# Counting edges between matmuls: two rings of one-hots and a new order of the three engines

## The chip, the cores and the metric

The kernel runs on one core of a Trainium2 chip. The metric is the device time of one execution in microseconds (us). Its engines are named as in the profile: PE is TensorE, DVE is VectorE, ACT is ScalarE, POOL is GpSimd, SP is SyncE, which issues most transfers.

## What is computed

Four graph layers over 1250 nodes with 512 features and 20000 edges `src -> dst`, `dst` sorted and dense at low numbers. Each layer normalises, aggregates over edges and multiplies by weights; two of them do so twice, so there are six convolutions (L0, L1A, L1B, L2, L3A, L3B).

```python
edge_index = jnp.stack([src, dst])
h = jnp.maximum(_layernorm(x, axis=-1), 0.0)
x = x + _L0_gnn_ref(h, edge_index, ...)   # relu(mean over edges of h @ W_l.T + b_l + h @ W_r.T)
h = jnp.maximum(_layernorm(x, axis=-1), 0.0)
x = x + _L1_gnn_ref(h, edge_index, ...)   # two convolutions
h = jnp.maximum(_layernorm(x, axis=-1), 0.0)
x = x + _L2_gnn_ref(h, edge_index, ...)
h = jnp.maximum(_layernorm(x, axis=-1), 0.0)
x = x + _L3_gnn_ref(h, edge_index, ...)   # two convolutions
return x
```

## The kernel before

The sum over edges is a product with a matrix of counts, nodes by nodes: entry (d, s) is how many edges go from s to d. The kernel builds this matrix once, while it also computes the two products of L0, and then aggregates six times with it.

**Counting.** The receivers are cut into 20 windows of 64 nodes, named (b, h): tile b of 128 nodes (0 to 9), h is 0 or 1. The 20000 sorted edges lie in 157 tiles of 128 edges. One stretch of counting is one window: `count(b, h)` on TensorE visits the tiles of edges that hold its receivers, in groups of six (RING): for each of the six, two matmuls of 320 columns take a one-hot of receivers (`dst_hot`, 128 columns: the window's nodes, once for the lower and once for the upper half of the senders) against a one-hot of senders (`src_hot`, 640 columns). The number of groups comes from a table, `tiles_of`, that the kernel computes itself; each engine loads a window's entry into a register (`visits_of`, the TENSOR_LOAD of line 254) and keeps in a register `visited` how many edge tiles are done. There are 35 groups: 6 and 3 in windows (0,0) and (0,1), two in each window of tiles 1 to 4, one in each of tiles 5 to 9. A window's counting begins with two matmuls of zeros (L1150) and ends with one (L1164).

Three engines share a group. VectorE (`givers`, L753 to L762) makes the six `src_hot` and the last two `dst_hot`; ScalarE (`receivers`, L486 to L496) the first four `dst_hot`, as 1 - |node - receiver| cut at zero: four times `apart` (L491), then one instruction over all four (L496). There is one ring of six buffers: `hot_used` counts the buffers that TensorE has read, and both makers wait for it. ScalarE's `counts_of` (L464) then moves the counts out of their two PSUM banks (4 and 5 for h = 0, 6 and 7 for h = 1) into `count16`, and SyncE transposes them by DMA into `countT16`.

**L0's products.** Per node tile b: ScalarE `deviation` (L477), VectorE `features` (normalised z, L781 and L788), TensorE `turn` (four transposes into PSUM, L1173), ScalarE `hi` (L514) and VectorE `lo` (L801) (the transposed features split into two parts), TensorE `first_p` (twelve matmuls, the neighbour product) and `first_q` (twelve, the own product, both L1180), ScalarE `phi` (L520) and VectorE `p_rest` (L808) (the product p split into two parts), VectorE `first_own` (L814). `statistics` (L735, L740, L744) are those of the next tile's rows.

**The order** is written out by hand for each engine; every engine runs in its own order and waits on semaphores. For tile b from 2 on, `merged(b, r)` has, on

- PE: count(b,0), first_p(b-1), turn(b), count(b,1), first_q(b-1)
- DVE: givers(b,0), features(b), first_own(b-2), givers(b,1), lo(b), statistics(b+1), p_rest(b-1)
- ACT: deviation(b), receivers(b,0), counts_of(b,0), receivers(b,1), hi(b), phi(b-1), counts_of(b,1)

in loops over pairs of tiles; tiles 0 and 1 come before the loop, mixed with the turning and splitting of L0's weights (`turn_first`, `split_first`). SyncE's list `order` has the transposes of tiles 0 and 1, the load of W1l into `wstage` (the weights of L1A, for which ScalarE waits at the start of L0's aggregation, L457), then the transposes of tiles 2 to 9, then three rows of vectors. After the last products the kernel reads one value (`big`) and branches; L0's aggregation is `aggregate` (L1259): 20 matmuls per tile against `cstage`, which ScalarE's `stage` (L529) writes for tile i + 2 when tile i is aggregated.

The wait that ties ScalarE's receivers to the ring:

```python
act.wait_ge(first_rows, n + RING)
for e in range(BY_ACT):
    last = nc.scalar.activation(apart[:, e:e + 1, :], tab[:, window(b, h), :], ACT.Abs, scale=-1.0,
                                bias=nodeT[:, 0, bass.ds(t + e, 1)])
last.then_inc(apart_done, RING)
act.wait_ge(apart_done, n + RING)
act.wait_ge(hot_used, n + BY_ACT)
nc.scalar.activation(dst_hot[:, 0:BY_ACT, :], apart[:, :, :], ACT.Relu, scale=-1.0,
                     bias=1.0).then_inc(first_rows, RING)
```

Of the kernel before, what the change touches and what calls it, by code (L numbers as in the profile page):

```python
# [13 lines left out]
P = 128  # L14
# [24 lines left out]
def gnn_kernel(nc, ins, out):  # L39
# [49 lines left out]
    wstage, _ = place("wstage", [P, KF, D], F32)  # L89
# [28 lines left out]
    apart, _ = place("apart", [P, BY_ACT, P], BF16, place.end)  # L118
# [35 lines left out]
    def p_bank(s, r):  # L154

        return PP if s == L0 else PP + r

    def q_bank(s, r):

        return PP + 1 if s == L0 else QQ + r  # L160
# [19 lines left out]
    givers_ready, hot_used = sem("givers_ready"), sem("hot_used")  # L180
    first_rows, ones_set = sem("first_rows"), sem("ones_set")
    apart_done, nodes_placed = sem("apart_done"), sem("nodes_placed")
# [69 lines left out]
    def visits_of(engine, visited, b, h):  # L252
# [4 lines left out]
        n0 = engine.snap(visited, min_val=0, max_val=NW * (ETP + RING))  # L257
# [3 lines left out]
        engine.reg_mov(visited, n1)  # L261
# [19 lines left out]
    with nc.Block() as block:  # L281

        @block.sync
        def _(sp):
# [15 lines left out]
            order = [("f", 0), ("f", 1), ("f", 2), ("v", rows[0]), ("v", rows[1]), ("t", 0), ("t", 1), loads[0]]  # L300
            order += [("t", b) for b in range(2, NT)]
# [127 lines left out]
        def _(act):  # L429
# [13 lines left out]
            act.sem_inc(first_rows, RING)  # L443
# [36 lines left out]
            visited = act.alloc_register("act_visited")  # L480
            act.reg_mov(visited, 0)

            def receivers(b, h):

                n0, n1, offset = visits_of(act, visited, b, h)
                with act.Fori(n0, n1, RING) as n:  # L486

                    t = tile_at(act, n, offset)
                    act.wait_ge(first_rows, n + RING)
                    for e in range(BY_ACT):  # L490
                        last = nc.scalar.activation(apart[:, e:e + 1, :], tab[:, window(b, h), :], ACT.Abs, scale=-1.0,  # L491
                                                    bias=nodeT[:, 0, bass.ds(t + e, 1)])
                    last.then_inc(apart_done, RING)
                    act.wait_ge(apart_done, n + RING)
                    act.wait_ge(hot_used, n + BY_ACT)
                    nc.scalar.activation(dst_hot[:, 0:BY_ACT, :], apart[:, :, :], ACT.Relu, scale=-1.0,  # L496
                                         bias=1.0).then_inc(first_rows, RING)
# [11 lines left out]
            def hi(s, i, r):  # L509
# [4 lines left out]
                nc.scalar.activation(hT_hi[:, r, :, :], ps[:, HT + r, :].rearrange("p (k n) -> p k n", k=KF),  # L514
# [22 lines left out]
            receivers(0, 0)  # L537
            split_first(0, range(2, KF))
            receivers(0, 1)
            counts_of(0, 0)  # L540
            split_first(1, range(0, 2))
            deviation(0, 0)
            deviation(0, 1)
            receivers(1, 0)
            counts_of(0, 1)
            split_first(1, range(2, KF))
            receivers(1, 1)
            counts_of(1, 0)
            hi(L0, 0, 0)
            phi(L0, 0, 0)  # L550
            hi(L0, 1, 1)
            counts_of(1, 1)
# [11 lines left out]
            with act.Fori(2, NT - 1, 2) as b0:  # L564
                for k in range(2):
                    merged(b0 + k, k)

# [739 lines left out]
```

## Time and profile before

| | |
|---|---|
| median of 3 runs | 703.03 us (702.97 to 704.32) |
| profiled execution | 705.11 us, span 703.3 us |
| TensorE busy | 662.6 us, 94% of the span |
| VectorE busy | 401.7 us, 57% |
| ScalarE busy | 283.1 us, 40% |
| counting and L0's products | from the start to 171.44 us |
| mean granted TensorE clock | 0.990 |

The span is the time from the first to the last instruction of the profiled execution; the device time of the same execution is 1.8 us more. A busy share near 100% over the whole span says nothing about one stage: the page's 40 slices have TensorE at 5 to 9 tenths in the first ten slices and at 9 from there on. A row of the timeline gives start, duration, instruction and, in brackets, how long the engine sat idle before it and whose work ended that. The array's matmuls overlap: twelve counting matmuls have a busy time of 1.80 us, but what follows can start 1.66 us after their start.

### The profile page before, as it was taken

The page shows a single profiled execution, that of the slowest core. Times are in us where ns is not written, and L with a number is a line of the kernel's source. Part 1 is how long each engine was busy: PE and PEld are TensorE (multiplying, and loading weights), DVE is VectorE, ACT ScalarE, POOL GpSimd, SP SyncE. Part 2 cuts the span into 40 slices and gives each one's busy share as a digit, 9 for nine tenths or more (in the row PEclk, how much of TensorE's full clock was granted, in tenths as well). Part 3 has the DMA queues.
Part 4 walks back from the last instruction along what each step waited for, and adds up shares of the span by engine and source line. Part 5 has one row for each costly group of instructions (what it writes and reads, how often), then busy time and mean ns, then how long its engine had stood idle before and what let it go on. Part 6 is the DMA issues. An engine that isn't in the chain of part 4 may idle for free.

```text
span 703.3 us, 11458 instructions
## 1 busy us (share of the span) xinstructions
PE 662.6 (94%) x3199; PEld 527.5 (75%) x3200; DVE 401.7 (57%) x911; ACT 283.1 (40%) x522; POOL 18.1 (3%) x25
## 2 busy tenths in 40 slices
PE   5878888988999999999999999999999999999997
PEld 3436566766888888888888888888877778887786
DVE  6986787674566444133434567554899861156323
ACT  4864665664341123563223332223553352223321
POOL 2000000000000000000000000000321000000000
PEclk9989999999999999999999999999999999999999
DMA  6213101113055000210000210000200000000011
GB/s 225 79 20 88 21 19 28 30 36 82 35 158 105 0 0 2 75 60 1 0 0 2 75 61 0 0 0 4 75 1 0 0 3 0 0 1 0 32 61 56
DMA packets 26273, 25.22 MB, mean 36 GB/s; under 512 B 14076, under 2 KB 17972, under 8 KB 26232
## 3 DMA queue, kind: packets, MB, share of 16 engines
q1 hardware_dynamic: 24952, 22.12, 11.2%
q10 hardware_dynamic: 1280, 2.56, 1.1%
q8 instruction: 24, 0.39, 0.2%
q14 instruction: 17, 0.14, 0.1%
HBM read 17.20 MB, written 4.20 MB: 30 GB/s over the span
## 4 chain that ended last, share of the span: by engine, by line
PE 80%; DVE 7%; issue 6%; ACT 3%; DVEq 2%; ACTq 0%; DMA 0%; SPq 0%
PE ps L1259 36%; PE ps L1180 33%; PE ps L1159 7%; PE ps L1173 3%; DVE src_hot L762 2%; DVE stats L735 1%; ACT cstage L529 1%; DVE own L994 1%; ACT dst_hot L496 1%; ACT apart L491 1%; PE ps L1121 1%; DVEq L762 0%; DVE mv_now L740 0%; DVE hT_lo L801 0%; DVE dst_hot L760 0%
## 5 line engine op out<-in xcount | busy, mean ns | idle before, releaser
L1259 PE MATMUL ps<-p_hi,cstage 128*128 128x512 f32 x600 | 235.7, 393 | 5.7 <-ACT cstage L529 2.9
L1259 PE MATMUL ps<-p_lo,cstage 128*128 128x512 f32 x600 | 234.6, 391 | 0.0
L1180 PE MATMUL ps<-w_hi,hT_hi 128*128 128x512 f32 x400 | 162.3, 406 | 3.4 <-DVE hT_lo L801 3.3
L1180 PE MATMUL ps<-w_hi,hT_lo 128*128 128x512 f32 x400 | 156.7, 392 | 0.0
L1180 PE MATMUL ps<-w_lo,hT_hi 128*128 128x512 f32 x400 | 156.2, 390 | 0.0
L1259 PEld LDWEIGHTS ps<-p_hi,cstage 128*128 128x128 f32 x600 | 113.2, 189 | 30.9 <-issue 7.3
L1259 PEld LDWEIGHTS ps<-p_lo,cstage 128*128 128x128 f32 x600 | 113.3, 189 | 23.1
L966 DVE SCALAR_TENSOR_TENSOR own<-ps,nodal,own 128x512 f32 (+1 forms) x60 | 44.9, 749 | 123.0 <-PE ps L1259 122.6
L529 ACT CAST cstage<-countT 128x1280 fp32r (+1 forms) x50 | 62.6, 1263 | 89.1 <-PE ps L1259 88.4
L1180 PEld LDWEIGHTS ps<-w_hi,hT_hi 128*128 128x128 f32 x400 | 75.2, 188 | 19.8 <-DVE hT_lo L801 2.9
L1159 PE MATMUL ps<-src_hot,dst_hot 128*128 128x320 bf16 x420 | 68.7, 315 | 22.2 <-ACT dst_hot L496 12.3
L1180 PEld LDWEIGHTS ps<-w_hi,hT_lo 128*128 128x128 f32 x400 | 75.1, 188 | 16.5
L1180 PEld LDWEIGHTS ps<-w_lo,hT_hi 128*128 128x128 f32 x400 | 75.4, 188 | 13.9
L762 DVE TENSOR_SCALAR src_hot<-iota,nodeT 128x640 bf16<-128x640 f16 x210 | 71.5, 381 | 15.1 <-PE ps L1159 8.8
L1159 PEld LDWEIGHTS ps<-src_hot,dst_hot 128*128 128x128 bf16 x420 | 38.6, 102 | 47.9 <-DVE src_hot L762 32.0
L514 ACT ACTIVATE hT_hi<-ps 128x512 fp32r<-128x512 f32 x60 | 35.7, 594 | 73.7 <-PE ps L1173 73.5
L808 DVE TENSOR_TENSOR p_lo<-ps,p_hi 128x512 f32 (+1 forms) x40 | 27.6, 691 | 59.0 <-ACT p_hi L520 58.9
L520 ACT ACTIVATE p_hi<-ps 128x512 f32 (+1 forms) x40 | 23.9, 597 | 72.4 <-PE ps L1180 72.4
L801 DVE SCALAR_TENSOR_TENSOR hT_lo<-ps,hT_hi 128x512 fp32r<-128x512 f32 x60 | 41.0, 684 | 13.5 <-ACT hT_hi L514 13.3
L491 ACT ACTIVATE apart<-tab,nodeT 128x128 bf16 (+1 forms) x140 | 44.8, 391 | 9.7 <-issue 5.5
L477 ACT ACTIVATE nodal<-mv,eps (+1 forms) x40 | 11.7, 294 | 67.4 <-DVE mv L744 67.4
L1173 PE MATMUL ps<-ident,z 128*128 128x128 f32 x240 | 36.0, 272 | 0.2 <-DVE z L788 0.2
(117 smaller groups left out, 450.8 us busy)
## 6 DMA issues: line engine op xcount, KB each, us to landing
x<-in_x ACTq DMA_DIRECT2D x1, 2304.0 KB
out_x<-x SPq DMA_DIRECT2D x9, 256.0 KB
wstage<-in_L_gnn_W SPq DMA_DIRECT2D x2, 1024.0 KB, 5.2
swap<-count SPq DMA_DIRECT2D x2, 800.0 KB, 8.6
count<-swap SPq DMA_DIRECT2D x2, 800.0 KB, 8.1
wstage<-in_L_gnn_W_l SPq DMA_DIRECT2D x2, 512.0 KB, 4.2
w_own<-in_L_gnn_W_r SPq DMA_DIRECT2D x1, 1024.0 KB, 11.2
vec<-in_L_gnn_b SPq DMA_DIRECT2D x4, 256.0 KB, 7.7
```

What stands on the lines that cost most here:

```text
L491: last = nc.scalar.activation(apart[:, e:e + 1, :], tab[:, window(b, h), :], ACT.Abs, scale=-1.0, bias=nodeT[:, 0, bass.ds(t + e, 1)])
L514: nc.scalar.activation(hT_hi[:, r, :, :], ps[:, HT + r, :].rearrange("p (k n) -> p k n", k=KF), ACT.Relu).then_inc(hi_done, 1)
L520: nc.scalar.activation(p_hi[:, bass.ds(i, 1), :], ps[:, p_bank(s, r), :], ACT.Copy, scale=1.0 if CONVS[s]["own"] else dis[:, bass.ds(i, 1) ...
L529: nc.scalar.copy(stage_of(s, r), columns(s, i)).then_inc(stage_ready, 1)
L762: nc.vector.tensor_scalar(src_hot[:, e, 0:NS], iota[:, :], nodeT[:, 1, bass.ds(t + e, 1)], None, ALU.is_equal).then_inc(givers_ready, 1)
L801: nc.vector.scalar_tensor_tensor(hT_lo[:, r, :, :], ps[:, HT + r, :].rearrange("p (k n) -> p k n", k=KF), 0.0, hT_hi[:, r, :, :].bitcast(F ...
L808: nc.vector.tensor_tensor(p_lo[:, bass.ds(i, 1), :], ps[:, p_bank(s, r), :], p_hi[:, bass.ds(i, 1), :].bitcast(F32), ALU.subtract).then_in ...
L966: nc.vector.scalar_tensor_tensor(own_, ps[:, AGG + r:AGG + r + 1, :], scale[:, bass.ds(i, 1)], own_, ALU.mult, ALU.add).then_inc(t_done, 1)
L1159: last = nc.tensor.matmul(ps[:, COUNT + 2 * h + k, 0:NS // 2], dst_hot[:, e, :], src_hot[:, e, k * (NS // 2):(k + 1) * (NS // 2)], start=F ...
L1173: last = nc.tensor.transpose(ps[:, HT + r, k * P:(k + 1) * P], z[:, r, k * P:(k + 1) * P], ident[:, :])
L1180: last = nc.tensor.matmul(ps[:, bank, :], a[:, r, k, :], w[:, slot, k, :], start=n == 0, stop=n == len(pairs) - 1)
L1259: last = nc.tensor.matmul(ps[:, AGG + r, :], cstage[:, part, k, :], p_[:, k, :], start=n == 1, stop=n == 2 * len(parts) * NT)
```

## The change

- `src_hot`, `dst_hot` and `apart` exist twice, and so do the semaphores `givers_ready`, `hot_used`, `first_rows`, `apart_done` and the register `visited`: windows with h = 0 use ring 0, windows with h = 1 ring 1. Ring 1's `src_hot` lies in `wstage`.
- The orders are rewritten. A step `merged` and a step `merged_end` make one tile; both end with the one-hots of the window after. `statistics` comes in its three parts, with the load from the table behind the first; elsewhere the load stands behind z, counts or ahead of the product.
- ScalarE moves a window's counts out after it has made the receivers of the next window, and `phi` and `p_rest` come one tile later.
- L0's PSUM banks: p has banks 1 and 2 by turns, q has bank 3, the turned features bank 0 alone; `turn` waits `lo` of the tile before, `first_p(i)` waits `p_rest(i-2)`.
- SyncE loads W1l after all transposes.
- Tiles 8 and 9 are written out behind the loop on all three engines (before: on VectorE alone).

```diff
-    src_hot, _ = place("src_hot", [P, RING, NS], BF16, cstage_at)
-    dst_hot, _ = place("dst_hot", [P, RING, P], BF16, place.end)
+    src_hot, dst_hot, apart = [None, None], [None, None], [None, None]
+    src_hot[0], _ = place("src_hot0", [P, RING, NS], BF16, cstage_at)
+    dst_hot[0], _ = place("dst_hot0", [P, RING, P], BF16, place.end)
+    apart[0], _ = place("apart0", [P, BY_ACT, P], BF16, place.end)
     assert place.end <= cstage_at + 2 * NT * P * 4
+    src_hot[1], _ = place("src_hot1", [P, RING, NS], BF16, wstage_at)
+    assert place.end <= wstage_at + KF * D * 4
+    dst_hot[1], _ = place("dst_hot1", [P, RING, P], BF16, own_at + 9 * D * 4)
...
-            order = [("f", 0), ("f", 1), ("f", 2), ("v", rows[0]), ("v", rows[1]), ("t", 0), ("t", 1), loads[0]]
-            order += [("t", b) for b in range(2, NT)]
+            order = [("f", 0), ("f", 1), ("f", 2), ("v", rows[0]), ("v", rows[1])]
+            order += [("t", b) for b in range(NT)] + loads[:1]
...
             def merged(b, r):
 
                 deviation(0, b)
-                receivers(b, 0)
+                counts_of(b - 1, 1)
+                found = visits_of(act, visited, b, 1)
+                phi(L0, b - 2, r)
+                receivers(b, 1, found)
                 counts_of(b, 0)
-                receivers(b, 1)
+
+            def merged_end(b, r):
+
+                found = visits_of(act, visited, b + 1, 0)
                 hi(L0, b, r)
-                phi(L0, b - 1, 1 - r)
-                counts_of(b, 1)
+                receivers(b + 1, 0, found)
...
+            givers(0, 1, visits_of(dve, visited, 0, 1))
             dve.wait_ge(x_loaded, 32)
-            statistics(0, 0)
+            statistics_1(0, 0)
+            found = visits_of(dve, visited, 1, 0)
+            statistics_2(0, 0)
+            statistics_3(0, 0)
             split_first(1, range(0, 2))
-            statistics(0, 1)
+            givers(1, 0, found)
             features(L0, 0, 0)
-            givers(1, 0)
...
             def merged(b, r):
 
-                givers(b, 0)
                 features(L0, b, r)
+                found = visits_of(dve, visited, b, 1)
+                p_rest(L0, b - 2, r)
                 first_own(b - 2)
-                givers(b, 1)
+                givers(b, 1, found)
+
+            def merged_end(b, r):
+
+                statistics_1(0, b + 1)
+                found = visits_of(dve, visited, b + 1, 0)
+                statistics_2(0, b + 1)
+                statistics_3(0, b + 1)
                 lo(L0, b, r)
-                if not (isinstance(b, int) and b == NT - 1):
-                    statistics(0, b + 1)
-                p_rest(L0, b - 1, 1 - r)
+                givers(b + 1, 0, found)
...
+            def merged(b, r):
+                found = visits_of(pe, visited, b, 1)
                 first_p(b - 1, 1 - r)
                 turn(L0, b, r)
-                count(b, 1)
+                count(b, 1, found)
...
+                found = visits_of(pe, visited, b + 1, 0)
                 first_q(b - 1, 1 - r)
+                count(b + 1, 0, found)
```

In the order of instructions two places matter. The first is ScalarE's, in the loop over tile pairs, from `hi` to the load ahead of the next window's receivers (names: `apart_79` below is the first of the two `apart`). Before:

```order
L514 ACTIVATE hT_hi<-ps 128x512
L519 REGISTER_ALU
L520 ISA
L520 ACTIVATE p_hi<-ps 128x512
L463 REGISTER_ALU
L464 ISA
L464 ACTIVATE count_49,deg_win<-ps 128x640
L477 ISA
L477 ACTIVATE nodal<-mv,eps 128x1
L254 ISA
L254 TENSOR_LOAD tiles_of
L257 ISA
```

And in the changed kernel, from `counts_of(b, 0)` on:

```order
L474 ACTIVATE count_49,deg_win<-ps 128x640
L263 ISA
L263 TENSOR_LOAD tiles_of
L266 ISA
L525 ACTIVATE hT_hi<-ps 128x512
L497 UNCONDITIONAL_BRANCH
L497 ISA
L502 ISA
L502 REGISTER_ALU
L502 ISA
L502 ACTIVATE apart_79<-tab,nodeT 128x128
```

Between `hi` of a tile and the first receivers of the next tile stood p_hi, the counts of (b,1), the deviation and the load; now nothing stands there but the branch into the ring's loop.

The second is VectorE's, in the same loop, from `lo` to the next tile's first one-hot of senders. Before:

```order
L801 SCALAR_TENSOR_TENSOR hT_lo<-ps,hT_hi 128x512
L735 ISA
L735 BN_STATS stats<-x 128x6
L738 REGISTER_ALU
L740 BN_AGGR mv_now<-stats 128x2
L744 ISA
L744 TENSOR_SCALAR mv<-mv_now 128x2
L808 ISA
L808 TENSOR_TENSOR p_lo<-ps,p_hi 128x512
L254 REGISTER_ALU
L254 TENSOR_LOAD tiles_of
L257 ISA
```

In the changed kernel:

```order
L759 BN_STATS stats<-x 128x6
L263 ISA
L263 TENSOR_LOAD tiles_of
L266 ISA
L764 BN_AGGR mv_now<-stats 128x2
L768 REGISTER_ALU
L768 TENSOR_SCALAR mv<-mv_now 128x2
L825 REGISTER_ALU
L826 SCALAR_TENSOR_TENSOR hT_lo<-ps,hT_hi 128x512
L778 UNCONDITIONAL_BRANCH
L778 ISA
L787 REGISTER_ALU
```

Statistics and the load moved ahead of `lo`, and `p_lo` went to the step `merged`, behind `features`.

## Rows read from the trace of the kernel before

**Rows 1.** Windows of the trace: busy time of each engine, granted clock, DMA share, GB/s

```profile
20.00:36.00 16.00, 13.31 (x90) 7.40 (x88) 15.50 (x54) 13.15 (x35) 0.00 (x0) 1.00 0.11 34
...
42.00:44.00 2.00, 1.36 (x6) 0.79 (x7) 1.23 (x5) 1.78 (x5) 0.00 (x0) 0.50 0.05 8
...
62.00:160.00 98.00, 86.66 (x521) 64.33 (x522) 73.56 (x234) 61.99 (x159) 0.00 (x0) 1.00 0.17 36
```

**Rows 2.** Waits up to 170 us: total us, times, longest

```profile
PE ps L1159 <- ACT dst_hot L496: 12.3, 11, 4.9
DVE hT_lo L801 <- ACT hT_hi L514: 12.1, 5, 2.8
PE ps L1159 <- DVE src_hot L762: 9.2, 11, 1.1
```

**Rows 3.** Timeline of TensorE, tiles 4 to 6: start, us, instruction, idle before

```profile
103.65 1.80 PE L1159 MATMUL ps<-src_hot,dst_hot 128*128 128x320 bf16 x12 [0.57 <-ACT dst_hot L496]
...
109.30 1.80 PE L1159 MATMUL ps<-src_hot,dst_hot 128*128 128x320 bf16 x12 [0.91 <-DVE src_hot L762]
...
114.52 1.80 PE L1159 MATMUL ps<-src_hot,dst_hot 128*128 128x320 bf16 x12
...
119.00 0.23 PE L1150 MATMUL ps<-zeros 128*128 128x64 bf16 x2
120.31 1.80 PE L1159 MATMUL ps<-src_hot,dst_hot 128*128 128x320 bf16 x12 [1.07 <-DVE src_hot L762]
```

**Rows 4.** Timeline of ScalarE ahead of the group at 120.31

```profile
116.50 0.70 ACT L464 ACTIVATE count<-ps 128x640 f32 x1 [0.97 <-PE ps L1164]
...
118.09 1.28 ACT L491 ACTIVATE apart<-tab,nodeT 128x128 bf16 x4 [0.61 <-issue]
119.54 0.63 ACT L496 ACTIVATE dst_hot<-apart 128x512 bf16<-128x512 bf16 x1 [0.17 <-ACT apart L491]
```

**Rows 5.** Timeline of VectorE, tiles 5, 6 and 9

```profile
106.99 1.28 DVE L762 TENSOR_SCALAR src_hot<-iota,nodeT 128x640 bf16<-128x640 f16 x4 [0.28 <-issue]
...
118.53 1.27 DVE L762 TENSOR_SCALAR src_hot<-iota,nodeT 128x640 bf16<-128x640 f16 x4 [0.85 <-issue]
...
120.63 0.15 DVE L781 RECIPROCAL nodal<-nodal  x1
...
158.95 0.69 DVE L801 SCALAR_TENSOR_TENSOR hT_lo<-ps,hT_hi 128x512 fp32r<-128x512 f32 x1 [2.79 <-ACT hT_hi L514]
```

**Rows 6.** Timeline of TensorE, tiles 1 to 4

```profile
42.64 6.26 PE L1159 MATMUL ps<-src_hot,dst_hot 128*128 128x320 bf16 x24 [4.92 <-ACT dst_hot L496]
...
55.30 0.50 PE L1180 MATMUL ps<-w_hi,hT_hi 128*128 128x512 f32 x1 [1.25 <-DVE hT_lo L801]
...
62.40 1.80 PE L1159 MATMUL ps<-src_hot,dst_hot 128*128 128x320 bf16 x12 [0.82 <-DVE src_hot L762]
...
93.79 1.80 PE L1159 MATMUL ps<-src_hot,dst_hot 128*128 128x320 bf16 x12 [0.96 <-DVE src_hot L762]
```

**Rows 7.** Timeline of VectorE, end of givers(0,1) and start of givers(1,0)

```profile
36.11 0.69 DVE L735 BATCH_NORM_STATS2 stats<-x 128x6 f32<-128x512 f32 x1
...
40.65 1.28 DVE L762 TENSOR_SCALAR src_hot<-iota,nodeT 128x640 bf16<-128x640 f16 x4 [0.34 <-issue]
```

**Rows 8.** Chain of waits at the end of the stage: start us, us, what

```profile
169.61 1.82 issue
171.44 42.60 PE ps L1259 x180
```

**Rows 9.** Timeline of ScalarE at the first aggregation: W1l's casts, the next stage

```profile
169.51 2.17 ACT L457 CAST w_hi<-wstage 128x512 fp32r<-128x512 f32 x4
177.92 1.26 ACT L529 CAST cstage<-countT 128x1280 fp32r x1 [6.24 <-PE ps L1259]
```

**Rows 10.** Timeline of SyncE's queue: the first load after the transposes

```profile
162.45 0.58 SPq L345 DMA_DIRECT2D vec<-in_L_gnn_b_neigh  x1
```

**Rows 11.** DMA view: issues of W1l's load, KB, us to landing

```profile
wstage<-in_L_gnn_W1l SPq DMA_DIRECT2D x1, 1024.0 KB, 5.4
```

More of the change, by code:

```diff
@@ L88, in gnn_kernel @@
     w_lo, _ = place("w_lo", [P, 2, KF, D], F32R)
-    wstage, _ = place("wstage", [P, KF, D], F32)
+    wstage, wstage_at = place("wstage", [P, KF, D], F32)
     z, z_at = place("z", [P, 2, D], F32)
@@ L117, in gnn_kernel @@
     zeros, _ = place("zeros", [P, P], BF16, place.end)
-    apart, _ = place("apart", [P, BY_ACT, P], BF16, place.end)
+    apart[1], _ = place("apart1", [P, BY_ACT, P], BF16, place.end)
     assert place.end <= relued_at + 2 * D * 4
@@ L179, in gnn_kernel @@
     w_loaded, wT_ready, whi_done, wlo_done = sem("w_loaded"), sem("wT_ready"), sem("whi_done"), sem("wlo_done")
[L180 to L182 removed]
+    givers_ready, hot_used, first_rows, apart_done = (
+        [sem(f"{what}{h}") for h in range(2)] for what in ("givers_ready", "hot_used", "first_rows", "apart_done"))
+    nodes_placed = sem("nodes_placed")
     counts_ready, counts_out, cT_loaded = sem("counts_ready"), sem("counts_out"), sem("cT_loaded")
@@ L442, in _ @@
             act.sem_inc(counts_out, 2)
-            act.sem_inc(first_rows, RING)
+            for s_ in first_rows:
+                act.sem_inc(s_, RING)
             act.sem_inc(deg_out_done, 1)
@@ L478, in deviation, with receivers @@
                                      bias=eps[:, 0:1]).then_inc(std_done, 1)
[L480 to L485, printed above, removed]
+            visited = [act.alloc_register(f"act_visited{h}") for h in range(2)]
+            for h in range(2):
+                act.reg_mov(visited[h], 0)
+            def receivers(b, h, found):
+                n0, n1, offset = found
                 with act.Fori(n0, n1, RING) as n:
                     t = tile_at(act, n, offset)
-                    act.wait_ge(first_rows, n + RING)
+                    act.wait_ge(first_rows[h], n + RING)
                     for e in range(BY_ACT):
[L491 to L497, printed above, removed]
+                        last = nc.scalar.activation(apart[h][:, e:e + 1, :], tab[:, window(b, h), :], ACT.Abs,
+                                                    scale=-1.0, bias=nodeT[:, 0, bass.ds(t + e, 1)])
+                    last.then_inc(apart_done[h], RING)
+                    act.wait_ge(apart_done[h], n + RING)
+                    act.wait_ge(hot_used[h], n + BY_ACT)
+                    nc.scalar.activation(dst_hot[h][:, 0:BY_ACT, :], apart[h][:, :, :], ACT.Relu, scale=-1.0,
+                                         bias=1.0).then_inc(first_rows[h], RING)
             act.wait_ge(table_pe, 2)
@@ L745, in statistics_3, with givers @@
                                         ALU.mult).then_inc(mv_done, 1)
-            visited = dve.alloc_register("dve_visited")
-            dve.reg_mov(visited, 0)
-            def givers(b, h):
-                n0, n1, offset = visits_of(dve, visited, b, h)
+            visited = [dve.alloc_register(f"dve_visited{h}") for h in range(2)]
+            for h in range(2):
+                dve.reg_mov(visited[h], 0)
+            def givers(b, h, found):
+                n0, n1, offset = found
                 with dve.Fori(n0, n1, RING) as n:
@@ L1083, in _ @@
         def _(pe):
-            pe.sem_inc(hot_used, RING)
+            for s_ in hot_used:
+                pe.sem_inc(s_, RING)
             for s_ in (zT_ready, p_ready, q_ready, agg_ready):
@@ L1141, in _, with count @@
             turn_first(0, (2, 3))
-            visited = pe.alloc_register("pe_visited")
-            pe.reg_mov(visited, 0)
-            def count(b, h):
+            visited = [pe.alloc_register(f"pe_visited{h}") for h in range(2)]
+            for h in range(2):
+                pe.reg_mov(visited[h], 0)
+            def count(b, h, found):
                 pe.wait_ge(counts_out, 2 * b + h + 1)
```

129 lines of the change are left out of this document (79 added, 50 removed).

## Prediction

> **What bounds it now.** I read the slices and windows first, then the waits, then the timeline of each engine. In the windows [rows 1] TensorE is busy 86.66 of the 98 us between 62 and 160, and VectorE and ScalarE stand at 73.56 and 61.99 of the same 98. So past 62 us the array is the bound with holes in it, and before that VectorE is (15.50 of 16 us from 20 to 36). The chain of waits has the start of the first aggregation at 171.44, after 1.82 us of "issue" [rows 8]; behind it the diff touches nothing: all that can move is the first 171 us.
>
> The waits [rows 2] say who makes the holes: counting matmuls (L1159) wait 12.3 us for ScalarE's dst_hot and 9.2 us for VectorE's src_hot. The view names one releaser of several, so I check it in the timelines. Take the hole of 1.07 us ahead of the group at 120.31 [rows 3]. ScalarE took the counts of the stretch before at 116.50, after idling 0.97 us for their end, then the deviation, then idled 0.61 us on the load from the table, then apart at 118.09 and dst_hot from 119.54 to 120.17 [rows 4]; the matmul starts 0.14 us later. The same 0.13 to 0.14 us lies between the end of dst_hot and the group after each hole, whichever engine is named. The cause is thus ScalarE's order: the count is moved out before the next receivers are made, so they can't be made ahead. VectorE sits idle in the same time, 12.1 us in five waits for hT_hi [rows 2].
>
> A dense tile (2 to 4) has four groups of one-hots, two to a stretch; its second group starts 0.57 us late (at 103.65) [rows 3]. This one is the ring itself: dst_hot can be overwritten only when four of the six matmul pairs have read it.
>
> **The change, part by part.**
> Two rings. The group after a change of stretch no longer waits for the last; the second group of one stretch still shares its ring, so I leave its six waits of 0.57 us (and those of the six groups of the very first stretch) as they are.
>
> Order. ScalarE now does hi, receivers(b+1,0), deviation, counts_of(b,1), phi, receivers(b,1): each set of receivers starts while TensorE still has a product ahead of it. Count from the end of turn(b), for a late tile. TensorE still has 0.28 us of opening zeros, count(b,1) from 114.52, first_q(b-1) to 119.00, and the next 0.2 us of zeros: some 4.9 us [rows 3]. Meanwhile hi ends at 0.6 us, receivers (1.28 + 0.17 + 0.63 us, rows 4) at 2.8 us; VectorE's lo ends at 1.3 us and its group takes 2.13 us (118.53 to 120.63) [rows 5], ending at 3.5 us. Both have over 1 us to spare, so the holes should close. Tiles 6 to 9 have one such hole each, 1.06 to 1.11 us [rows 3]: **4.3 us**. In the dense tiles four holes, 0.91, 0.26, 0.96 and 0.91 us: **3.0 us** [rows 3, 6]. There the margin is thinner: after its second group, VectorE still has statistics (1.3 us) and lo (0.7 us) to do before the first sender of the next stretch; with the hi that lo waits for, the sender comes about 0.5 us before TensorE asks for it; I take it as covered, but this is where I would lose part of the 3.0.
>
> Does another engine become the bound? A late tile took 11.01 us (109.30 to 120.31) and should take 9.9; a dense one 15.5 (93.79 to 109.30) less 0.91, 14.6 [rows 3, 6]. From 62 to 160 VectorE is busy 73.56 us and ScalarE 61.99 [rows 1]; in a stretch shorter by 7.3 us, 90.7, that is 81% and 68%, with the register loads on top (0.3 to 0.85 us for each of 16 stretches, rows 5) at most 96% and 83% if none were hidden. TensorE stays the bound.
>
> Loads of the table. Now behind bn_stats, z, counts or a product; VectorE's exposed 0.28 and 0.85 us [rows 5] go. They are on no path once the groups are ahead: nothing in the sum.
>
> The start. VectorE decides it. It is through with givers(0,1) at 36.11 [rows 7] in both. Before, two statistics, w_lo twice, and features stand ahead of givers(1,0), which starts at 40.65 [rows 7], and TensorE starts at 42.64 after 4.92 us of nothing [rows 6]. Now one statistics (1.2 us) and w_lo (1.2 us): I put the first src_hot at 38.9 and the first matmul at 39.4. From there at VectorE's pace (2.13 us a group): givers(1,0) to 43.2; features and statistics to 45.3; givers(1,1) to 49.7; lo to 50.3; first_p 50.4 to 53.3 and turn to 53.7; hi and lo by 55.0 and the first sender of (2,0) by 55.5, while first_q runs to 56.5. With the zeros count(2,0) starts at 56.7, where it started at 62.40 [rows 6]: **5.7 us**.
>
> In this walk the groups run at full clock. Before, after the 4.92 us of idling, the granted clock is 0.50, the 1.2 GHz level, and the two groups take 6.26 us where VectorE's pace would give 4.3 [rows 1, 6]. After 1.25 us of idling the matmul at 55.30 took 0.50 us [rows 6], as the first of such a product does elsewhere: the clock had stayed up. The new idle stretch is 1.7 us, nearer to the latter; so 0, with 1.9 us as the bad end. The Trainium skill, "TensorE: Matmul & The Clock Gate", Part 1, speaks against me: an array that has idled is served at half rate until it has been busy for a while. By it the start would be worth 1.9 us less and the time 692; the trace shows both outcomes.
>
> Banks. L0 now has p in two banks, q in one, turned features in one. turn(b) waits lo(b-1), which first_p(b-1), just ahead of it, waits for anyway. first_p(b-1) waits only p_lo(b-3). Nothing.
>
> W1l. Its load goes behind the last transposes (its place in wstage is now the second ring): on the old time axis it would be issued where the vec loads begin, at 162.45, and with its 5.4 us land at 167.9; ScalarE reads it at 169.51 [rows 9 to 11]. Even at twice those 5.4 us the four casts (2.17 us) end at 175.4, and the next stage waits until 177.92 in any case. Nothing.
>
> Tail. TensorE runs first_q, first_p and first_q, then the If; the 1.82 us of "issue" stay [rows 8].
>
> Sum: 5.7 + 3.0 + 4.3 = **13.0 us**. The profiled execution took 705.11 us (span 703.3); that gives 692.1. It stands 2.1 us above the median of 703.03; against that, **690.0 us**.
>
> **Rivals.**
> A, the start doesn't gain: VectorE or a late w_lo eats what is moved. For it: VectorE is busy 15.50 of 16 us from 20 to 36 [rows 1]. Against: from 37.7 to 42.64 TensorE is empty. Then only 7.3 us: 695.7. Chance 0.12.
>
> B, code: the loops are longer, and tiles 8 and 9 are written out on TensorE and ScalarE. What the engine's own issue costs is 0.57 us more at VectorE's loop turn (0.85 against 0.28, rows 5), and 1.82 us at the If [rows 8]. At three turns and one exit on the array itself, 4 x 1.8 = 7.3 us lost: 697.3. Against: TensorE's loop turn shows no such gap before. Chance 0.06. The Trainium skill, "Runtime: NRT & Kernel Launch", Instruction fetch mechanics, has this rule: a taken branch out of the stretch held by the engine stalls until it is fetched.
>
> C, slower: lo now stands directly ahead of givers(b+1,0), and hi on ScalarE behind receivers(b,1), counts_of(b,0) and a load. If this chain from turn to the first sender is over 4.9 us, TensorE waits after every first_q, 8 times. At the longest wait seen for hT_hi, 2.79 us [rows 5], that is 22.3 us against 13.0: 712.3. For it: VectorE waited for hi in five tiles. Against: it came early then, and hi followed the turn by 0.1 us. Chance 0.05.
>
> D, nothing: the holes are filled, but others open of the same size, since each engine is in order: 703. Chance 0.06.
>
> E, more: the handovers around the zeros (0.1 to 0.3 us at 18 stretches) and part of the 0.57 us shrink: under 688. Chance 0.05.
>
> **Numbers.** Forecast 0.66. The range runs from E's edge, 688.0, over the clock's 1.9 us and lost margin in the dense tiles, to A, 696.5; it leaves out B, C, D and part of E. About 0.2%, 1.4 us, is what the measurement can tell from no change. Faster: forecast, A, B and E, 0.89; within it D, 0.06; slower C, 0.05.
>
> **What would show it.** First counting matmul of (1,0) near 39.4, of (2,0) near 57, of (5,0) near 101, the first aggregating one near 158.4 instead of 171.44. Idle ahead of the counting matmuls from 22.2 to about 11 us. No hole after any first_q; late tiles at 9.9 us and dense ones at 14.6. The clock at 40 to 46 us tells of the 1.9. W1l must land before ScalarE's first w_hi of the next convolution. Late tiles still at 11 us would make the forecast wrong; so would a start at 60 or later.

## The result, and the profile after

The changed kernel takes **694.64 us** (median of 4 runs, 693.88 to 695.33) against 703.67 us for the kernel before, run on the same chip (4 runs, 702.97 to 704.64): ratio 0.9871, interval 0.9852 to 0.9889. That is 9.0 us less where I had forecast 13.0. The time lies in the range, faster was right, but the size was off by 4 us. The profiled execution took 694.39 us (span 692.6, mean clock 0.994); before, it was 705.11 (span 703.3). The comparison below is between these two.

**Counting gained more than I had said.** Windows of the trace after (columns as in [rows 1]):

```profile
42.00:44.00 2.00, 0.99 (x9) 0.56 (x7) 1.57 (x5) 1.70 (x5) 0.00 (x0) 1.00 0.40 80
62.00:144.00 82.00, 79.79 (x492) 59.90 (x491) 66.75 (x213) 54.48 (x145) 0.00 (x0) 1.00 0.15 31
```

From 62 us to the end of counting TensorE is now busy 79.79 us of 82, where it was 86.66 of 98 [rows 1]: the holes shrank from 11.3 to 2.2 us. VectorE is at 81%, ScalarE at 66%. The waits up to 170 us:

```profile
DVE hT_lo L826 <- ACT hT_hi L525: 7.5, 5, 2.7
...
PE ps L1204 <- ACT dst_hot L507: 5.0, 9, 1.9
```

ScalarE held the counting matmuls back for 12.3 us before [rows 2] and for 5.0 now. TensorE's timeline, from tile 1 on:

```profile
37.81 4.35 PE L1204 MATMUL ps<-src_hot,dst_hot 128*128 128x320 bf16 x24 [1.11 <-DVE src_hot L787]
...
65.05 1.80 PE L1204 MATMUL ps<-src_hot,dst_hot 128*128 128x320 bf16 x12 [0.32 <-ACT dst_hot L507]
...
98.50 1.79 PE L1204 MATMUL ps<-src_hot,dst_hot 128*128 128x320 bf16 x12
...
103.47 1.79 PE L1204 MATMUL ps<-src_hot,dst_hot 128*128 128x320 bf16 x12
...
107.95 0.23 PE L1196 MATMUL ps<-zeros 128*128 128x64 bf16 x2
108.02 1.79 PE L1204 MATMUL ps<-src_hot,dst_hot 128*128 128x320 bf16 x12
```

Here 98.50 is (5,0), which answers to 109.30 [rows 3], 103.47 is (5,1), 108.02 is (6,0). The hole of 1.07 us behind the product is gone, and the opening zeros overlap what follows: they start 0.07 us ahead of the counting matmuls. A late tile takes 9.52 us instead of 11.01. The last stretch ends at 143.35 instead of 160.24, where the last product of L0 starts: **16.9 us**.

ScalarE in the same tile:

```profile
103.61 0.60 ACT L525 ACTIVATE hT_hi<-ps 128x512 fp32r<-128x512 f32 x1 [2.34 <-PE ps L1218]
104.10 1.27 ACT L502 ACTIVATE apart<-tab,nodeT 128x128 bf16 x4
105.54 0.63 ACT L507 ACTIVATE dst_hot<-apart 128x512 bf16<-128x512 bf16 x1 [0.17 <-ACT apart L502]
106.23 0.30 ACT L487 ACTIVATE nodal<-mv,eps  x1
106.53 0.70 ACT L474 ACTIVATE count<-ps 128x640 f32 x1
```

The receivers of (6,0) are ready at 106.17, 1.85 us before TensorE reads them. The counts follow; before, they stood ahead [rows 4].

**Some 6 us were given back behind counting.** First at the branch ahead of L0's aggregation. The chain of waits:

```profile
151.77 1.26 ACT cstage L540
153.03 3.07 issue
156.10 4.11 PE ps L1319 x11
```

The matmul at 156.10 starts after 4.34 us in which TensorE is idle (2.79 before), and the "issue" in the chain was 1.82 us [rows 8] and is 3.07. From the end of counting to the first aggregating matmul it was 11.20 us and is 12.75: 1.5 us lost. Then in L3A, 400 us further on, in code that the diff does not touch. TensorE's timeline before, and after:

```profile
574.02 0.47 PE L1259 MATMUL ps<-p_hi,cstage 128*128 128x512 f32 x1 [1.14 <-ACT cstage L529]
574.33 0.39 PE L1259 MATMUL ps<-p_lo,cstage 128*128 128x512 f32 x1
574.55 0.40 PE L1259 MATMUL ps<-p_hi,cstage 128*128 128x512 f32 x1
```

```profile
559.11 0.47 PE L1319 MATMUL ps<-p_hi,cstage 128*128 128x512 f32 x1 [1.14 <-ACT cstage L540]
559.42 0.40 PE L1319 MATMUL ps<-p_lo,cstage 128*128 128x512 f32 x1
562.04 0.80 PE L1319 MATMUL ps<-p_hi,cstage 128*128 128x512 f32 x1 [2.23 <-issue]
```

Two matmuls, then 2.23 us of nothing, then one of twice the duration and, behind it, matmuls that start 0.43 us after each other instead of 0.23. The windows say why these are slow:

```profile
560.00:562.00 2.00, 0.00 (x0) 0.00 (x0) 2.00 (x4) 0.94 (x2) 0.00 (x0) 0.95 0.00 0
562.00:564.00 2.00, 1.96 (x5) 1.57 (x6) 0.72 (x2) 0.00 (x0) 0.00 (x0) 0.50 0.03 8
564.00:566.00 2.00, 2.00 (x8) 1.58 (x7) 0.00 (x0) 0.00 (x0) 0.00 (x0) 0.70 0.00 0
```

The granted clock fell to 0.50, the 1.2 GHz level, after this idle stretch. L3B's first aggregation started 79.41 us after L3A's before (574.02 to 653.43) and 83.55 us after (559.11 to 642.66): 4.1 us lost. The page's groups show it in one line each, before and after (the last field is idle time ahead of them):

```profile
L1259 PE MATMUL ps<-p_hi,cstage 128*128 128x512 f32 x600 | 235.7, 393 | 5.7 <-ACT cstage L529 2.9
```

```profile
L1319 PE MATMUL ps<-p_hi,cstage 128*128 128x512 f32 x600 | 236.6, 394 | 9.9 <-issue 6.6
```

The account closes: 16.9 gained, less 1.5 at the branch, less 4.1 in L3A, less 0.5 elsewhere (0.43 us between the two and 0.07 behind L3B's start), is 10.8 of the 10.7 us by which the span shrank.

### The profile page after: what moved, and what is told of

The parts are those of the page before. It is cut to its first block, busy times and chain, and to the rows that moved or that the text cites. A ratio compares the mean times of both kernels' runs of the same rounds, so it can differ in the third digit from the quotient of the medians.

```text
span 692.6 us, 11472 instructions
## 1 busy us (share of the span) xinstructions
PE 660.0 (95%) x3199; PEld 525.4 (76%) x3200; DVE 399.5 (58%) x911; ACT 280.4 (40%) x522; POOL 18.1 (3%) x25
## 3 DMA queue, kind: packets, MB, share of 16 engines
q1 hardware_dynamic: 24952, 22.12, 11.3%
## 4 chain that ended last, share of the span: by engine, by line
PE 86%; issue 5%; DVE 4%; ACT 2%; DVEq 1%; DMA 1%; ACTq 0%; SPq 0%
PE ps L1225 38%; PE ps L1319 37%; PE ps L1204 7%; PE ps L1218 3%; ACT cstage L540 1%; DVE src_hot L787 1%; ACT dst_hot L507 1%; DVE own L1038 1%; DMA wstage<-in_L_gnn_W_l 1%; PE ps L1166 1%; DVE stats L759 0%; DVE own L1010 0%; DVE own L862 0%; DVE mv_now L764 0%; DVE x L1047 0%
## 5 line engine op out<-in xcount | busy, mean ns | idle before, releaser
L1204 PE MATMUL ps<-src_hot,dst_hot 128*128 128x320 bf16 x420 | 65.0, 300 | 9.8 <-ACT dst_hot L507 5.0
L1204 PEld LDWEIGHTS ps<-src_hot,dst_hot 128*128 128x128 bf16 x420 | 36.6, 98 | 32.4 <-DVE src_hot L787 20.6
L502 ACT ACTIVATE apart<-tab,nodeT 128x128 bf16<-128x128 f16 (+1 forms) x140 | 44.6, 392 | 3.6 <-ACT dst_hot L507 3.6
```

The costliest lines, as they stand in the source:

```text
L502: last = nc.scalar.activation(apart[h][:, e:e + 1, :], tab[:, window(b, h), :], ACT.Abs, scale=-1.0, bias=nodeT[:, 0, bass.ds(t + e, 1)])
L1204: last = nc.tensor.matmul(ps[:, COUNT + 2 * h + k, 0:NS // 2], dst_hot[h][:, e, :], src_hot[h][:, e, k * (NS // 2):(k + 1) * (NS // 2)], s ...
```

## Theories

About the given-back time I had two, and they do not exclude each other. **Code:** the "issue" would be TensorE waiting for its own instructions. The DMA view of 556 to 566 us has no data transfer at all, only this:

```profile
q8 instruction: 3, 0.05, 2.1%
```

Three packets of 16 KB each of instructions. The Trainium skill, "Runtime: NRT & Kernel Launch", Instruction fetch mechanics, says that instructions come in such blocks, 256 instructions each, ahead of use and in sequence, and that a taken branch to a block not held stalls. The packets' size agrees with it; whether the rest does is what the experiments ask. The change makes TensorE's code ahead of the branches longer by 298 instructions (tiles 8 and 9 written out; a matmul counts as two, since the trace lists a weight load for each: PEld x3200, PE x3199), so that by a count over the program the target of L3A's branch moved from place 173 in its block of 256 to place 215, near the end: what follows the target is soon in another block. **Transfers:** W1l's load and three vectors now stand in flight while TensorE branches. About the gain I asked which part made it: the second ring, ScalarE's order, or the loads' place.

## The experiments

Every ratio is to the kernel before, run on the same chip as the variant (its median 704.87 us beside the first four, 705.41, 704.64 and 705.60 beside the others). In all of them `tiles_of` is held as U16, which control_after, the changed kernel with that alone, shows to cost nothing (694.20 us); beyond that each differs from its base by the edit shown. I compare the variants with each other, mostly by their traces.

**1. Code that is never executed.** The added increments sit in the side of L0's branch that is not taken.

```diff
                 with pe.If(big > 0):
+                    if s == L0:
+                        for _ in range(64):      # 42 in the kernel before; 256 in after_pad256
+                            pe.sem_inc(sem("never"), 1)
                     aggregate_all(lambda r: (0, 1))
```

> The changed kernel with 64 instructions put on TensorE into the branch that is never taken (large counts, L0), so that nothing more is executed and all of TensorE's later code stands 64 instructions further on. Theory 1, code fetch: the 2.23 us of issue behind the second matmul of L3A's first aggregation, and the half clock behind it, come from where a block of code ends behind that branch; they go (about 4 us), and of the 4.34 us ahead of L0's first aggregation at least 1.5 us go as well: 689 to 690.5 us. Theory 2, transfers: L0's longer wait comes from W1l's load being in flight at that moment; then only L3A's 4 us go, 690.5 to 691. Theory 3, neither: 694.6 us as before.

> The kernel before with 42 instructions in the same never-taken branch, which puts TensorE's later code at the same remainder of 256 instructions as in the changed kernel. Theory 1: the stall behind the second matmul of L3A's aggregation appears here too, about 4 us, and 1.5 us ahead of L0's first aggregation: 707.5 to 709.5 us. Theory 2: 707.5, L0's wait stays at 2.8 us. Theory 3: 703.7 us.

> The changed kernel with 256 instead of 64 never-executed instructions at the same place: in TensorE's code (a matmul counted as two instructions) everything behind them stands 256 later, so at the same place modulo 256 as in the changed kernel. Theory 'the place of the branch's target within a block of 256 instructions': the stop of 2.2 us two matmuls into L3A's first aggregation and the half clock after it are back, 694.4 within 1 us. Rival 'any longer jump or any other layout does it': no stop, 690.2 within 1 us, as with 64.

> The changed kernel itself, with the small table tiles_of held as U16 instead of I32, as in all variants. Every theory: no difference from the changed kernel, 694.6 us, within 1 us. In its profile: a stop of about 2.2 us two matmuls into L3A's first aggregation near 559 us, the first aggregation of L0 near 156.1.

| | us | ratio, interval | place of L3A's target | stop in L3A |
|---|---|---|---|---|
| control_after | 694.20 | 0.9846 (0.9814 to 0.9878) | 215 | 1.95 us |
| after_pad64 | 690.18 | 0.9790 (0.9762 to 0.9818) | 23 | none |
| after_pad256 | 695.80 | 0.9878 (0.9861 to 0.9894) | 215 | 1.75 us |
| before | 704.87 | | 173 | none |
| before_pad42 | 709.21 | 1.0056 (1.0036 to 1.0077) | 215 | see below |

With 64 instructions that never run, TensorE's timeline in L3A reads:

```profile
559.59 0.40 PE L1319 MATMUL ps<-p_lo,cstage 128*128 128x512 f32 x1
559.82 0.39 PE L1319 MATMUL ps<-p_hi,cstage 128*128 128x512 f32 x1
```

With 256, which shift the code by one whole block, the stop is back, at the same matmul:

```profile
559.21 0.40 PE L1319 MATMUL ps<-p_lo,cstage 128*128 128x512 f32 x1
561.36 0.50 PE L1319 MATMUL ps<-p_hi,cstage 128*128 128x512 f32 x1 [1.75 <-issue]
```

And 42 of them in the kernel before bring a wait that it never had, ahead of the first matmul; its clock then fell to 0.50 as well (window 578 to 580):

```profile
576.65 0.50 PE L1259 MATMUL ps<-p_hi,cstage 128*128 128x512 f32 x1 [3.57 <-issue]
```

What decides here is where the code stands in its blocks: 64 more instructions take the stop away, 256 bring it back, and 42 bring one to a kernel that had none. (That the period is 256 is the block's size; by the runs alone it could be 128 too.) The stop costs 1.8 to 2.2 us by itself: in before_pad42 the data were ready at 574.78, and 1.87 of its 3.57 us are "issue". From L3A's first aggregation to L3B's it is 79.41 us before and 79.68 with the 64 instructions, 81.73 and 81.84 in control_after and after_pad256, whose clock stayed at 1.00 behind the stop, and 83.55 in the changed kernel, whose clock didn't.

The instruction queue says what is waited for. In windows of 0.1 us, a packet of q8 comes at 556.2 and a second at 559.3 in the changed kernel, and the matmul behind the stop starts at 562.04. In control_after the second comes at 560.6 and the matmul at 563.06, in after_pad256 at 559.1 and 561.36, in before_pad42 at 574.3 and 576.65: always 2.3 to 2.7 us behind it, whether that is the third matmul or the first. With 64 instructions the second packet comes as well (559.5), and nothing waits for it.

Two things the rule does not give. By the same count L1A's target stands at 206 in the changed kernel and L1B's at 221 in the kernel before, and neither has a stop; why L3A's has one is open. And the wait at L0's branch, of which this theory had at least 1.5 us go with the 64 instructions, stays: 3.66 us against 3.83 in control_after, and 2.80 in before_pad42 against 2.79. Moved code is not its cause.

**2. W1l's load after the branch.** SyncE waits until ScalarE's first stages of L0 are done (each kernel also with the 64 instructions: after_late_pad64).

```diff
                     sp.wait_ge(wlo_done, KF * what)
+                    if what == 2:
+                        sp.wait_ge(stage_ready, tile(L0, 1))
```

> The changed kernel with SyncE loading W1l and the three vectors only when ScalarE has staged tile 1 of L0 (some 8 us later), so that no transfer is in flight while TensorE branches. The casts of W1l end some 2 us before the next stage is due. Theory 1: L0's wait of 4.34 us stays, 694.6 us. Theory 2: it falls to 2.8 us: 693.1 us. If W1l then comes too late, ScalarE's next stage and the third aggregation are late: above 695.

> Both together. Theory 1: as with the 64 instructions alone, 689 to 690.5. Theory 2: 689 to 689.5, with the 64 alone 1.5 us above it.

690.87 us (0.9799, 0.9774 to 0.9825) and 688.16 us (0.9763, 0.9726 to 0.9800). The chain of waits of after_late:

```profile
152.86 1.26 ACT cstage L542
154.12 1.30 issue
155.42 1.63 PE ps L1321 x6
```

1.30 instead of 3.07 us of "issue"; in L3A its stop of 2.23 us is still there, and with the 64 instructions it is gone. So there are two causes. The kernel came out 2.2 us below the 693.1 that I had expected of a shorter wait alone: the clock also stayed at 1.00 in the window 156 to 160 us, where the changed kernel had 0.62 after its longer wait. That is no sure gain: in after_late_pad64's profiled execution the clock fell to 0.50 (window 158 to 160) after 2.60 us of idling. ScalarE now waits for W1l in the open, and nothing is later for it:

```profile
160.79 2.18 ACT L469 CAST w_hi<-wstage 128x512 fp32r<-128x512 f32 x4 [6.68 <-DMA wstage<-in_L_gnn_W1l]
162.88 1.26 ACT L542 CAST cstage<-countT 128x1280 fp32r x1
```

**3. One ring, new order** (with the 64 instructions): buffers, semaphores and `visited` of ring 1 are those of ring 0, all else as changed.

```diff
-    src_hot[1], _ = place("src_hot1", [P, RING, NS], BF16, wstage_at)
-    dst_hot[1], _ = place("dst_hot1", [P, RING, P], BF16, own_at + 9 * D * 4)
-    apart[1], _ = place("apart1", [P, BY_ACT, P], BF16, place.end)
+    src_hot[1], dst_hot[1] = src_hot[0], dst_hot[0]
+    apart[1] = apart[0]
```

> The changed order of the three engines, but one ring of six one-hots with one set of semaphores, plus the 64 never-executed instructions; to be read against the changed kernel with these 64, 690.2 us. Theory 'the order did it' (my prediction named ScalarE's order as the cause of the holes): the makers still come ahead of the chores, and only the last buffers of the stretch before hold them; in dense tiles the group after a change of stretch then starts some 0.6 us late like a second group of one ring: 10 such handovers in tiles 1 to 4, and 0.3 to 0.5 us in each of the late ones; 690.2 + 3 to 6 = 693 to 696. Rival 'the second ring did it': with one ring the makers can't run ahead at all, counting falls back to its old pace and the kernel to the 7 to 13 us it had gained: 699 to 703. Rival 'the ring is worth nothing': 690.2, within 0.7.

692.11 us (0.9809, 0.9776 to 0.9842) against 690.18. The counting matmuls tell more than the two times. One ring, tiles 1 and 6 (second stretch of tile 1, first of tile 6):

```profile
45.94 4.42 PE L1200 MATMUL ps<-src_hot,dst_hot 128*128 128x320 bf16 x24 [0.95 <-DVE src_hot L784]
...
109.67 1.79 PE L1200 MATMUL ps<-src_hot,dst_hot 128*128 128x320 bf16 x12
```

Two rings:

```profile
45.48 4.42 PE L1204 MATMUL ps<-src_hot,dst_hot 128*128 128x320 bf16 x24 [0.95 <-DVE src_hot L787]
...
109.12 1.79 PE L1204 MATMUL ps<-src_hot,dst_hot 128*128 128x320 bf16 x12
```

63.73 and 63.64 us. The second ring is worth nothing to counting; my expectation of 3 to 6 us fell. One ring does hold ScalarE longer (its dst_hot waits 17.8 us for TensorE up to 170 us, 14.0 with two), but none of that reaches TensorE: from tile 2 on a product stands between any two stretches, before the change as after it, and it gives the makers time. The intervals of the two ratios overlap; what difference there is lies at the branch, where this run waited 4.78 us.

**4. Two rings, old order.** The buffers of the change and its late load of W1l, every engine's order and the banks as before.

> Two rings, their semaphores and the late load of W1l, but every engine in its old order, old banks. Its never-taken code stands as in the kernel before (no new stop in L3A). Theory 'the order did it': the holes of 0.9 to 1.1 us after each product stay, since counts, deviation and the load still stand ahead of the receivers; only the second stretch of a tile gains where VectorE or ScalarE waited for the ring: 0 to 2 us less than before, less 1 us for W1l's load at the branch: ratio 0.997 to 1.002. Rival 'the second ring did it': ratio 0.985 to 0.99. A start still at 42.6 us for count(1,0) and at 62 for count(2,0) in both.

706.73 us, ratio 1.0016 (1.0003 to 1.0030). The holes are all there:

```profile
108.08 1.80 PE L1169 MATMUL ps<-src_hot,dst_hot 128*128 128x320 bf16 x12 [0.90 <-DVE src_hot L770]
...
119.05 1.80 PE L1169 MATMUL ps<-src_hot,dst_hot 128*128 128x320 bf16 x12 [1.01 <-DVE src_hot L770]
```

Between these two groups lie 10.97 us, as before the change (11.01). The order did it. And the wait at the branch is 3.56 us where it was 2.79 before: the late load costs in the old order too.

**5. The loads from the table back in front of their loops**, on all engines (64 instructions).

> The changed kernel plus the 64 never-executed instructions, with each load from the table put back directly ahead of its loop, on all three engines; to be read against 690.2. My prediction gave the loads' place nothing. Theory 'nothing': 690.2 within 0.7. Rival 'on the path on TensorE': its load of about 0.5 us then stands between the opening zeros and the first counting matmul of each of 16 stretches; 4 to 8 us more, 694 to 698, with 'issue' gaps of 0.3 to 0.6 us ahead of the counting matmuls. On VectorE and ScalarE the load costs 0.3 to 0.85 us of idle in either theory, hidden in the late tiles.

690.54 us (0.9783, 0.9750 to 0.9816): the same as after_pad64. But in the traces two effects work against each other. At the start (1,1) waits 1.50 us instead of 0.95. From there to (6,0) it gains 1.3 us (62.34 against 63.64): in the changed kernel TensorE's load stands between a stretch and the product behind it. The changed kernel, and the one with loads in front:

```profile
59.59 0.47 PE L1225 MATMUL ps<-w_hi,hT_hi 128*128 128x512 f32 x1 [0.53 <-issue]
```

```profile
60.99 0.19 PE L1200 MATMUL ps<-zeros 128*128 128x64 bf16 x1
61.22 0.47 PE L1216 MATMUL ps<-w_hi,hT_hi 128*128 128x512 f32 x1
```

The changed kernel has such a gap of 0.5 us at two of the six dense stretches (59.59 and 88.35) and smaller ones at the others; with the load directly ahead of its own stretch 0.2 us are left at the first and none at the others.

**6. One ring, W1l's load at its old place** (possible, since `wstage` is free again), and then with the loads from the table in front in the loops alone; both with the 64 instructions.

```diff
-            order += [("t", b) for b in range(NT)] + loads[:1]
+            order += [("t", 0), ("t", 1), loads[0]]
+            order += [("t", b) for b in range(2, NT)]
...
-                found = visits_of(pe, visited, b, 1)
                 first_p(b - 1, 1 - r)
                 turn(L0, b, r)
-                count(b, 1, found)
+                count(b, 1, visits_of(pe, visited, b, 1))
```

> The changed order with one ring and the 64 never-executed instructions; since ring 1 no longer lies in wstage, W1l's load stands again behind the transposes of tiles 0 and 1. Theory 'the transfers in flight lengthen the wait at the branch': TensorE's wait ahead of L0's first aggregation falls from 4.78 us in the run with the late load to 2.6 to 2.8 us, the kernel from 692.1 to about 690, at best to the 688.2 of the version with two rings and a delayed load. Rival 'one ring itself costs 2 us there': wait stays over 3.5 us, 692. Counting as before: 63.7 us from the second group pair of (1,1) to the last group of tile 6 in both.

> As one_ring_early, and in the loops over tiles 2 to 9 each load from the table stands directly ahead of its stretch again, on all three engines; the loads of tiles 0 and 1 stay behind long instructions. From the run with all loads in front, where counting from (1,1) to tile 6 took 62.3 instead of 63.6 us but (1,1) began 0.5 us later: 1.3 us less than one_ring_early, without the 0.5 us. Theory 'the exit from a stretch to a product waits for the load on TensorE': 1.3 us less. Rival 'the difference was between executions': none.

688.49 us (0.9775, 0.9759 to 0.9792) and **686.98 us** (0.9750, 0.9734 to 0.9766), the fastest of the study, with less memory than the change. The 1.3 us expected of the loads came as 1.5. The wait at the branch, chain of one_ring_early:

```profile
152.78 1.26 ACT cstage L538
154.04 1.10 issue
155.14 9.99 PE ps L1316 x43
```

**7. ScalarE's order alone put back**, on one_ring_early, from tile 2 on; only `phi` keeps its new place.

```diff
             def merged(b, r):

-                deviation(0, b)
-                counts_of(b - 1, 1)
-                found = visits_of(act, visited, b, 1)
                 phi(L0, b - 2, r)
-                receivers(b, 1, found)
                 counts_of(b, 0)
+                receivers(b, 1, visits_of(act, visited, b, 1))
...
-                found = visits_of(act, visited, b + 1, 0)
                 hi(L0, b, r)
-                receivers(b + 1, 0, found)
+                counts_of(b, 1)
+                deviation(0, b + 1)
+                receivers(b + 1, 0, visits_of(act, visited, b + 1, 0))
```

> As one_ring_early, but from tile 2 on ScalarE's order is again the old one where my prediction saw the cause: the counts of the stretch just ended, the deviation and the load from the table stand ahead of the next receivers; VectorE and TensorE keep the new order. Theory 'ScalarE's order made the holes': the holes of 0.9 to 1.1 us behind each product are back, tiles 5 to 9 take again 10.5 to 11 us instead of 9.5 and the dense ones about 1 us more than now; 688.5 + 6 to 8 = 694.5 to 696.5, with the idle time ended by ScalarE's dst_hot. Rival 'VectorE made them': nothing comes back, 688.5 within 0.7. Rival 'only the load and the deviation count, the counts alone are covered by the product': holes of 0.3 to 0.5 us, 690 to 692.5.

696.42 us, ratio 0.9860 (0.9828 to 0.9891), 7.9 us more. TensorE's timeline, tiles 6 and 7:

```profile
103.19 1.80 PE L1201 MATMUL ps<-src_hot,dst_hot 128*128 128x320 bf16 x12 [0.47 <-ACT dst_hot L505]
...
113.70 1.80 PE L1201 MATMUL ps<-src_hot,dst_hot 128*128 128x320 bf16 x12 [0.56 <-ACT dst_hot L505]
```

A late tile takes 10.51 us. From (1,1) to the end of counting it is 105.7 us (46.06 to 151.76) against 99.2 (45.19 to 144.35): 6.5 us, of the 11.4 us that this part gained by the change (49.60 to 160.24, and 44.14 to 143.35). ScalarE's order is thus more than half of the gain there. The holes are half as long as before; the other half is what VectorE's and TensorE's new orders do, which no run took apart. The rest of the 7.9 us lies outside this part, some of it behind counting, where the clock was 0.50 in the window 164 to 166 of this execution and 1.00 in one_ring_early's there. In the dense tiles the second group's wait is 0.57 us again.

## Why the prediction was right and wrong

- **What bounds, and the cause:** right. ScalarE's order was the larger part (experiment 7). The second ring, which I had listed as a part of the cure, was none (experiments 3 and 4).
- **The start, 5.7 us:** (2,0) began at 54.94 instead of 62.40, 7.5 us earlier; in control_after at 56.01, 6.4. The walk from givers(0,1)'s end to the first sender was 2.8 us (36.11 to 38.9) and took 2.3 (35.06 to 37.38); the execution itself was 1.05 us ahead there already, which is chance between executions and not the change: control_after has 36.15. The clock stayed at 1.00 as assumed (window 42 to 44). The rule that I had cited against it (the Trainium skill, "TensorE: Matmul & The Clock Gate", Part 1) did not bite after 1.11 us of idling; in L3A the clock fell after 2.23 us of it in two executions and stayed up after 1.75 and 1.95 us in two others. How long TensorE idles does not settle it alone: after the same 2.38 us at L0's branch the clock stayed at 1.00 in one_ring_early and fell to 0.58 in one_ring_early_loads.
- **Dense tiles, 3.0 us:** (2,0) to (5,0) takes 43.56 us instead of 46.90: 3.3. That is near, and partly luck. The four holes closed, which is the 3.0 us; the second groups gave some 1.3 us that I had left out, and the overlapping zeros some 0.9; and the gaps behind the stretches (experiment 5), which I had put at nothing, took some 1.9 back. Two of the four holes in the kernel before:

```profile
77.93 1.80 PE L1159 MATMUL ps<-src_hot,dst_hot 128*128 128x320 bf16 x12 [0.91 <-DVE src_hot L762]
...
85.70 1.80 PE L1159 MATMUL ps<-src_hot,dst_hot 128*128 128x320 bf16 x12 [0.26 <-ACT dst_hot L496]
```

- **Late tiles, 4.3 us, mis-sized:** (5,0) to (9,0) takes 38.06 us instead of 43.90: 5.8. The step that failed is "late tiles 9.9": I kept the 0.1 to 0.3 us around the zeros at each stretch, but with the one-hots ready they overlap as well. That was rival E, on a small scale.
- **"This one is the ring itself", 0.57 us: wrong.** It was ScalarE's pace: a group takes it 0.29 + 1.28 + 0.17 + 0.63 = 2.37 us, which is 1.80 + 0.57. Now the second group's `apart` is ready early (its dst_hot waits 1.5 to 2.3 us for TensorE in the dense tiles), and the wait of TensorE is 0.32 us, with one ring and with two alike. That is what the ring itself costs.
- **Loads from the table, nothing:** wrong, though the sum came out right in experiment 5: behind long instructions at the start they gain 0.5 us, behind the stretches they lose 1.3, and putting back only the latter took 1.5 us off (experiment 6).
- **W1l, "nothing": wrong, and not in the way I checked.** ScalarE did have it in time. I asked only when it lands, not what else is under way while it moves: TensorE's fetch behind the branch. Moving it back (experiment 6) or further on (experiment 2) takes 1.1 to 2.4 us off the wait there (3.66 to 2.60, 4.34 to 2.58, 4.78 to 2.38).
- **"Tail: the 1.82 us of issue stay", and all behind 171.44 unmoved: wrong.** This is the step that decided the size. The diff does not touch the code there, but moves it. Rival B, with its rule from the Trainium skill, had the right kind of cost and looked for it at the counting loops' turns; small gaps of 0.5 us do stand there, but they are the load's. It was at the branch targets of the aggregations. B's price of 7.3 us was near the 5.6 us lost there; the mechanism I gave it did not happen.

The forecast's gain in counting was 3.9 us too small, and its loss behind counting (none) 6.2 us too small; the one error hid most of the other. That the time fell inside my range owes something to that luck.

## What to carry to other kernels

When an edit lengthens an engine's program, everything behind it moves in its blocks of code, and here a branch target that came to stand near the end of a block cost 2 to 4 us far from the edit: measure a variant with some never-executed instructions before judging the edit itself. Put the chores (moving results out, small preparations) behind the making of the next inputs, and only then ask whether another buffer is needed; here it was not. And look at what a moved transfer runs beside, not only at when it lands.

## What the runs showed of the hardware

The wait at L0's branch falls into two groups. Where W1l's load and the three vectors are in flight at the branch it is 3.56 to 4.78 us (seven runs: the changed kernel 4.34, control_after 3.83, after_pad64 3.66, after_pad256 3.89, one_ring_pad64 4.78, loads_front_pad64 3.83, old_order 3.56); where W1l is not, 2.38 to 2.80 us (before 2.79, before_pad42 2.80, after_late 2.58, after_late_pad64 2.60, one_ring_early 2.38, one_ring_early_loads 2.38, act_old_order 2.54). In the windows of one microsecond the aggregation starts some 2.7 to 2.9 us after the DMA share drops from about 1 (after: traffic until 153.2, start at 156.10; one_ring_pad64: until 155.4, start at 158.20; old_order: until 168.0, start at 170.86). The instruction queue shows the same from its side (q8's packet at the branch, in windows of 0.1 us, and the first aggregating matmul):

| | last matmul ends | q8's packet | matmul starts |
|---|---|---|---|
| after | 151.76 | 153.0 | 156.10 |
| one_ring_pad64 | 153.42 | 155.3 | 158.20 |
| old_order | 167.30 | 167.9 | 170.86 |
| before | 168.65 | 168.1 | 171.44 |
| after_late | 152.84 | 152.2 | 155.42 |
| one_ring_early | 152.76 | 152.2 | 155.14 |

From the packet to the matmul it is 2.9 to 3.3 us in all six; what differs is when the packet comes: 0.5 to 0.7 us ahead of the last matmul's end where W1l is not in flight, and 0.6 to 1.9 us behind it, as the data traffic ends, where it is. So the fetch comes late because of the data; whether it waits in the same engines or in memory no run here tells. Nor was it tried where the stop in L3A begins: L3A's target at 215 stopped in all kernels that have it there, and at 15 to 23, 173 and 175 in none.
